# Four of eight mixer blocks (silus and late projections) placed last in their slot instead of first

## The reference, cut to what matters

```
def ffn(x):                                   # _L1_ffn_ref, twice
    h = x = layernorm(x)
    for blk in range(3):
        y = h @ W[2*blk].T + b                # dequantized weight, low-rank part
        y = gelu(layernorm(y) * gamma + beta)
        h = y @ W[2*blk+1].T + b + h
    return h
def mixer(x):                                 # _L1_attn_b_ref, between the two FFNs
    xin = layernorm(x)
    xn = xin / (rms(xin) + 1e-8)
    u, v = silu(xn @ Wu.T + bu), silu(xn @ Wv.T + bv)      # 256 features each
    o[n] = sum(coef[lag] * v[n - lag] for lag in 0..n)     # over the batch axis, n = 0..7
    return (u * o) @ Wo.T + bo + xin
x = x + ffn(x); x = x + mixer(x); x = x + ffn(x)
```

## Time and profile before

| | us |
|---|---|
| median of 3 runs | 1559.68 (1559.05 to 1560.17) |
| the profiled execution | 1559.52 |
| its span, first to last instruction | 1557.6 |
| TensorE busy | 1305.2 (84%) |
| VectorE busy | 1029.0 (66%) |
| ScalarE busy | 831.8 (53%) |
| GpSimd busy | 841.0 (54%) |
| mean granted clock of TensorE, share of full speed | 0.93 |

### The profile page before, as it was taken

The page is one execution under the profiler, slowest core; times in us unless marked ns, Lnnn a source line. Parts: engine busy times, 40 slices in busy tenths (PEclk is TensorE's granted clock), DMA queues, the critical chain, the costliest instruction groups (busy, mean ns, idle before and its releaser), DMA issues. The chain is left out here.

```text
span 1557.6 us, 33714 instructions
## 1 busy us (share of the span) xinstructions
PE 1305.2 (84%) x11257; PEld 846.7 (54%) x11257; DVE 1029.0 (66%) x3074; ACT 831.8 (53%) x1425; POOL 841.0 (54%) x1254
## 2 busy tenths in 40 slices
PE   5775899887999999978899379899999978786678
PEld 4665889832344444448899233434455546544456
DVE  5765445457789888745454769887666526647976
ACT  3642123212677777742232258788555557777665
POOL 4465554434346655655554668887444205646543
PEclk9976899988999999979999679999999997988999
DMA  8012222176323333142221300000000000000001
GB/s 243 20 40 60 67 59 76 55 159 131 76 76 88 89 89 89 38 125 68 78 70 54 113 1 2 1 2 2 1 2 2 2 1 1 2 1 1 1 1 55
DMA packets 86437, 79.41 MB, mean 51 GB/s; under 512 B 11791, under 2 KB 76175, under 8 KB 85968
## 3 DMA queue, kind: packets, MB, share of 16 engines
q1 hardware_dynamic: 72434, 55.07, 14.2%
q0 software_dynamic: 8640, 17.84, 3.5%
q10 hardware_dynamic: 5196, 4.35, 1.2%
HBM read 45.94 MB, written 31.28 MB: 50 GB/s over the span
## 5 line engine op out<-in xcount | busy, mean ns | idle before, releaser
L1469 ACT ACTIVATE grp_pt<-ps 128x1024 f32<-128x1024 f32 (+2 forms) x320 | 243.9, 800 | 141.6 <-PE ps L1556 78.1
L2497 DVE TENSOR_REDUCE soft_mx<-ps 128x2 f32<-128x1024 f32 (+3 forms) x256 | 199.3, 818 | 36.3 <-PE ps L2283 34.7
L1042 POOL DMA_INDIRECT products<-moe_product,moe_rows_in x142 | 137.7, 970 | 146.9 <-DVE moe_product L1144 136.7
L2158 ACT ACTIVATE arena<-ps 128x768 f32<-128x768 f32 (+1 forms) x192 | 167.1, 881 | 83.6 <-PE ps L2316 67.5
L1061 ACT ACTIVATE moe_hid<-ps 128x512 f32<-128x512 f32 x142 | 84.3, 597 | 225.3 <-issue 111.3
L1092 PE MATMUL ps<-moe_rT,moe_W_now 128*128 128x128 f32 x1136 | 161.2, 288 | 11.2 <-DVE moe_rT L1136 7.1
L2059 POOL TENSOR_SCALAR_AFFINE_SELECT arena<-arena 128x256 f32<-128x256 f32 (+1 forms) x192 | 93.4, 488 | 123.0 <-ACT arena L2158 122.1
L1092 PEld LDWEIGHTS ps<-moe_rT,moe_W_now 128*128 128x128 f32 x1136 | 147.6, 203 | 14.8 <-DVE moe_rT L1136 7.5
L861 POOL DMA_INDIRECT sorted_rows<-route_row,route_target x128 | 126.1, 985 | 43.1 <-issue 30.4
L1571 PE MATMUL ps<-grp_pt,grp_vpad 128*32 128x160 f32 (+4 forms) x2048 | 139.9, 381 | 1.8 <-POOL grp_pt L1403 1.6
L1403 POOL TENSOR_SCALAR_AFFINE_SELECT grp_pt<-grp_pt 128x256 f32<-128x256 f32 (+1 forms) x192 | 111.8, 594 | 34.7 <-ACT grp_pt L1469 33.4
(11 more groups left out here) (375 smaller groups left out, 2856.4 us busy)
## 6 DMA issues: line engine op xcount, KB each, us to landing
moe_rows_in<-sorted_rows SPq DMA_DIRECT2D x142, 65.0 KB
route_stacks<-soft_scratch_k SPq DMA_DIRECT2D x32, 192.0 KB
arena<-products SPq DMA_DIRECT2D x8, 512.0 KB, 7.3
soft_scratch_q<-soft_parts SPq DMA_DIRECT2D x16, 192.0 KB, 2.7
route_stacks<-soft_scratch_q SPq DMA_DIRECT2D x32, 96.0 KB
arena<-products SPq DMA_DIRECT2D x4, 768.0 KB, 12.6
soft_scratch_k<-soft_parts SPq DMA_DIRECT2D x15, 192.0 KB, 2.7
products<-moe_product,moe_rows_in POOLq DMA_INDIRECT x142
```

The lines of the kernel that those rows point to most:

```text
L1042: pool.indirect_dma_start(k.products, bass.IndirectOffsetOnAxis(rows_in[:, s % RING, DEST_COL:DEST_COL + 1].bitcast(U32), 0), product[:, s ...
L1469: act.activation(at.pair(pt[:, s % 2, :], pair, seg)[:, :, 0:w], ring[(chunks_before(m) + c) % 2][:, :, 0:w], ACT.Exp, scale=scale).then_i ...
L2158: act.activation(LATENT.pair(pt[:, s % 2, :], pair, seg)[:, :, 0:w], ring[second_turn(n, c) % RING3][:, :, 0:w], ACT.Exp, scale=scale).the ...
L2497: ins = dve.tensor_reduce(mx[:, tile, half, :, r], ring[first_turn(n, d) % RING3][:, :, at:at + keys], AX.X, ALU.max)
```

## The change

The set `SILU_FIRST` names the batches whose block keeps its place, 2 to 5. For batches 0, 1, 6 and 7 (slots 20, 22, 33 and 35) ScalarE's `silu` goes to the end of the slot, behind `norm_mix`, and TensorE's late projections go to the end of the slot too, behind `project_uv` 0 and 1. The lists of VectorE, GpSimd and SyncE, the number of instructions and what they compute stay as they are.

```diff
     FIRST, END = -4, SLOTS + 6
+    SILU_FIRST = (2, 3, 4, 5)
...
             for t in range(FIRST, END):
-                if t - 5 in mixes:
+                if t - 5 in mixes and mixes[t - 5] in SILU_FIRST:
                     silu(mixes[t - 5])
                 if unit_at(t - 1):
                     scale(unit_no[FFN[t - 1]])
...
                 if t - 1 in mixes:
                     norm_mix(mixes[t - 1])
+                if t - 5 in mixes and mixes[t - 5] not in SILU_FIRST:
+                    silu(mixes[t - 5])
...
             for t in range(FIRST, END):
-                if t - 5 in mixes:
+                if t - 5 in mixes and mixes[t - 5] in SILU_FIRST:
                     project_uv(mixes[t - 5], 2)
                     project_uv(mixes[t - 5], 3)
                 if unit_at(t - 3):
...
                 if t - 4 in mixes:
                     project_uv(mixes[t - 4], 0)
                     project_uv(mixes[t - 4], 1)
+                if t - 5 in mixes and mixes[t - 5] not in SILU_FIRST:
+                    project_uv(mixes[t - 5], 2)
+                    project_uv(mixes[t - 5], 3)
```

## The result

The changed kernel took 1547.05 us (1546.01 to 1548.20, 4 runs), the kernel before 1559.37 us (1556.13 to 1560.17, 4 runs) in the same comparison: ratio 0.9934, 95% interval [0.9913, 0.9956]. The medians differ by 12.3 us, where 6.0 were forecast, and the time is outside the stated range of 1551 to 1558. By the ratio it is 10.3 us, with an interval from 6.9 to 13.6.

The account below looks back on a forecast made before the run. No engine is full (TensorE leads with 84%); waits between engines in the last stage, `tail`, were taken as the bound. 4.1 (batches 0 and 1) plus 1.9 (batches 6 and 7) made 6.0 us: 1559.52 to 1553.5, range 1551.0 to 1558.0.

Parts of the forecast that it names:

- the sum: Whole kernel: 4.1 + 1.9 = 6.0 us off the profiled 1559.52, giving 1553.5 us.
- Batch 1, forecast 4.1 with batch 0: Slots 22 and 23: 3.64 of wait and 1.5 of shorter block, less 0.6 and 0.5, make 4.1 us earlier.
- The bound for a slow clock (1.1): Batch 1, slot 22: at the slow clock output projection and block are 3.0 us worse, leaving 1.1 of 4.1.
- Batch 0, forecast +0.6: Slot 20: moved block stays slow at 6.2 to 6.3 us; ScalarE ends slot 21 0.6 us later, bounds 0 and +0.6.
- Batches 6 and 7, forecast 1.9 and 0: Slot 33: VectorE's waits for batch 5's output projection go, 1.9 us (bounds 0, 2.2); slot 35: 0 (bounds 0, +1.0).
- my chain: Slot 33: step-by-step ScalarE times, with batch 7's copy releasing batch 5's output projection at 1466.5 instead of 1472.05.
- No change: Rival, chance 0.12: one slot later is the same list, gaps only move to other waits; 1559.5 us.
- slower: Rival, chance 0.08: POOL sets the pace at slots 20 to 22, blocks of batches 0 and 1 start 4.25 later; 1566.1 us.
- Slow clock in batch 1: Rival, chance 0.14: batch 1's block and the output projection run at 1.2 GHz; gain 3.0 us, 1556.5 us.
- More: Rival, chance 0.12: batch 2's block turns fast too, 6.0 + 1.6, 1551.9 us; against it, TensorE would idle 2.6 us before.

Follow-up runs that it names:

- only_b0: Only the block of batch 0 (slot 20) moved, against the kernel before: ratio 1.0012 [0.9990, 1.0033]; last stage 274.99 us.
- only_b01: Only the blocks of batches 0 and 1 moved, 6 and 7 first as in the kernel before: last stage 271.39 us, against 275.36 before.
- only_b67: Only the blocks of batches 6 and 7 (slots 33 and 35) moved, against the kernel before: ratio 0.9996 [0.9974, 1.0017]; last stage 275.16 us.
- none_moved: All eight batches in SILU_FIRST, the order of the kernel before, run again: last stage 275.06 us, against 275.36 in the first trace.
- warm_unmoved: Order of the kernel before plus products of zeros ahead of late projections of batches 0, 1, 2, 4, 7 (18, 13, 9, 9, 9): 1554.08 us, ratio 0.9965.
- after_third: The changed kernel unaltered, run a third time against the kernel before: 1552.17 us against 1560.02, ratio 0.9953 [0.9933, 0.9973]; last stage 266.80 us.
- warm_more: The changed kernel plus products of zeros ahead of late projections of batches 0, 2, 4, 7 (20, 9, 9, 9): 1549.12 us, ratio 0.9924; last stage 263.71.
- warm: The changed kernel plus products of zeros ahead of late projections of batches 0, 2, 4 (20, 9, 6): 1524.46 us, ratio 0.9931; last stage 265.55.

## Why the prediction was wrong

**The step that failed is the sum.** It read "The profiled execution took 1559.52 ... 1553.5 us" and gave a range of 1551.0 to 1558.0, whose ends came from the edited stage alone. It had no term for the 1282 us ahead of that stage, as if they stayed as they were; the three runs on hand lay within 1.1 us. The runs showed in its place that these stages differ between executions by more than the whole forecast. In the first comparison 6.96 of the 13.1 us between the two traces were of this kind, 6.4 of them there by 220, in the first mixture of experts, with no edit ahead of it. On one chip 35 runs of the kernel before went from 1526.84 to 1542.22, and among the traces of four kernels there the last stage began between 1253.5 and 1262.0 us, 8.5 apart.

The three comparisons don't contradict each other: 6.9 to 13.6 us, 1.2 to 7.8 and 4.2 to 10.5 by their intervals, which have 6.9 to 7.8 in common. So the 12.3 between two medians of 4 runs is most likely too much, and by them the edit is worth some 7 us; the last stages of the three traces are 6.1, 6.2 and 8.6 us shorter than that of the first trace before. Why the first pair drew apart in just that way stays open: it wasn't tried what sets the pace of the two mixtures of experts, the chip of the first comparison isn't known (the kernel before took 1534.7, 1534.5 and 1560.0 us on three chips), and 4 runs of each may simply have fallen so.

**Batch 1, forecast 4.1 with batch 0: measured 4.6.** The wait of 3.64 us went. The block came out at 4.75 instead of 6.54, as priced; with the clock full on both sides the order alone is worth 3.15 (3.64 less 0.6 and 0.5 were 2.5 by my steps). The bound for a slow clock (1.1) didn't come up in three traces of the kernel.

**Batch 0, forecast +0.6: nothing in the sum of the stage (274.99 us in only_b0, 275.36 and 275.06 unmoved).** Its block stayed at 6.15 to 6.54; TensorE had idled 5.2 us before it. By the Trainium skill, "TensorE: Matmul & The Clock Gate", section "What's actually happening", the slow clock is the default and activity lifts it; the 20 products of zeros, which brought 6.54 down to 4.74, agree.

**Batches 6 and 7, forecast 1.9 and 0: 1.95 and 0 in slots 34 to 36 against the first trace, with luck in the 1.95.** The mechanism held: wherever batch 6 is moved, VectorE's addition of batch 5 waits for nothing, and no lag product waits for a silu. But the size of the wait that goes is itself set by the clock of the output projection. In the six traces with these batches unmoved it was 1.58, 0.68, 0.72, 0.57, 2.35 and 2.12 us; against only_b01 the move gives 0.95 in these slots. The forecast took the one wait that it had seen as fixed. What my chain had wrong inside: the entry of batch 4 waited 2.17 us for GpSimd, so the copy of batch 7 came 4.4 us earlier and not 5.6, and the output projection ran slow. Neither mattered, since VectorE is full there. Alone the pair is worth 0.2 us, as batch 7's block then met the low clock; behind batches 0 and 1 it brings the stage from 271.39 to 269.2.

**What cancelled.** By slot 34 the changed kernel was only 3.0 us ahead, where 4.1 were forecast, and from there to the end it won 3.1, where 1.9 were. The 1.60 lost between slots 24 and 34 is a term that my sum didn't have. In the first trace of before batch 4's block had the full clock (4.75), and so had the output projection of batch 3 behind it; in the changed kernel the block took 5.70 and the output projection 3.16 us. The first row is of before, the second of the changed kernel:

```profile
1439.09 1.95 PE L2919 MATMUL ps<-pack,tail_gated 128*128 128x128 f32 x16
```

```profile
1427.90 3.16 PE L2922 MATMUL ps<-pack,tail_gated 128*128 128x128 f32 x16
```

All kernels but only_b67 lose 1.59 or more there, none_moved with the old order 2.59, and warm_unmoved, with that order too, 1.59. So it isn't a cost of the order alone. But no kernel that moves batch 0 or 1 escaped it, and two of the four that leave them did (before and only_b67), so whether the edit makes the slow case likelier isn't known. The 1.17 at the end is the clock as well: at slot 38 VectorE waited 1.44 us for `first`, not 2.23, and `first` took 1.12 us, not 1.91. The close match of 6.16 with 6.0 is in part such luck: after_third has 8.56.

**The rivals.** No change and slower are out. "Slow clock in batch 1" didn't occur. "More" did, in after_third, where batch 2's block was fast; the argument against it, that TensorE would idle 2.6 us before that block, didn't decide: it idled 2.95 us there, and 2.95 in the first trace after, where the block was slow.

## What to carry to other kernels

An item at the end of one slot is the item ahead of the next: price such a move by what the neighbours wait for, above all a copy that frees a bank and stands behind the moved block. When a latency chain of two engines recurs, look at each occurrence's length; where equal ones differ (here 4.75 and 6.5 us), find what the clock does before crediting an order. A wait that you want to remove may have a length that the clock sets: read it in more than one trace before you price it (here 0.6 to 2.4 us for the same wait). And take the noise of the stages that the edit doesn't touch from more than three runs, or compare stage by stage: half of a measured gain may lie ahead of the first edited line.

## What the runs showed of the hardware

- The last stage repeated to 0.05 us in two executions of one kernel in different comparisons, and differed by 2.4 in a third. The two largest of the steps by which it differed are at places where TensorE's clock was low in the one and full in the other: late projections of 3.34 against 1.98 us, `second` of 2.07 against 1.12.
- Idle spells don't decide by their length alone whether the next matmuls are slow: 1.97 us was followed by passes at the full clock (1.98 us for four), 1.94 by 2.99 us, and in only_b0 one of 2.61 by 1.98 us. The same spell of the same kernel, 2.95 us, was followed by 3.34 us in one execution and by 1.98 in another.
- 20 matmuls of zeros in idle time, 4.49 us in all, delayed nothing (slot 21 begins where it does without them, within 0.01 us) and gave back 1.8 us at batch 0. Nine of them at batch 7 made its block fast and the stage no shorter (warm_more against warm, from slot 20 on).
